# A two-layer decoder on one core: values of the first attention inside its heads, Toeplitz rows in the first stage, the convolution's operands and more of the early projection in the feed-forward

## What is computed

```python
# layer 0, attention (H = 16 heads of 16)
g = x @ Wg.T + bg
v = x @ Wv.T + bv
corr = dot(g, g) / (nrm_i * nrm_j + 1e-08)       # per head, masked to j <= i
corr = (corr + 1.0) / 2.0
denom = mean(corr, axis=3) + 0.5
gene_fitness = 1.0 / (denom * sum(1.0 / denom, axis=2))
attn = softmax(corr * gene_fitness[..., None] * m + (1.0 - m) * NEG)
out = (attn @ v) @ Wo.T + bo

# layer 1, moving average of the normalised input (p, a, q: 256 x 16)
p, a = sigmoid(ema_delta), sigmoid(ema_alpha)
q = 1.0 - p * a
kern = p * ema_beta * exp(t * log(q))
k_dl = einsum('dnl,dn->dl', kern, ema_gamma * sqrt(1 / 16))
conv = causal convolution of xn with k_dl over the 32 steps of t
mx = silu(conv + xn * ema_omega)

# layer 1, cross-attention: keys and values of the context
k = (K @ Wk.T + bk)          # 4096 x 1024
v = (V @ Wv.T + bv)          # 4096 x 1024
```

## Time and profile before

| what | us |
|---|---|
| median of three runs | 2650.11 (2647.54 to 2652.91) |
| the profiled execution | 2642.07, its span 2640.2 |
| projection | 0 to 80.4 |
| heads | 80.4 to 495.2 |
| cross-attention of layer 0 | 495.2 to 868.2 |
| feed-forward | 868.2 to 1000.1 |
| convolution | 1000.2 to 1212.8 |
| gated attention and all behind it | 1212.8 to 2640.2 |

### The profile page before, as it was taken

One profiled execution on the slowest core, in us unless ns is written; L12 is line 12 of the kernel. 1 busy time (PEld: TensorE's weight loads), 2 busy tenths in 40 slices (PEclk: granted clock), 3 DMA queues, 4 the chain that ended last, 5 costly groups with the idle time before them and its releaser, 6 DMA issues. The chain is left out here.

```text
span 2640.2 us, 44590 instructions
## 1 busy us (share of the span) xinstructions
PE 2322.6 (88%) x17186; PEld 1783.3 (68%) x17186; DVE 1347.6 (51%) x2515; ACT 1131.5 (43%) x1934; POOL 845.9 (32%) x881
## 2 busy tenths in 40 slices
PE   9688888699998778698989869999999699999994
...
GB/s 76 79 103 121 122 102 131 92 33 25 31 67 17 182 195 225 128 210 136 32 32 64 24 130 54 111 113 101 99 120 91 216 203 181 180 198 173 183 223 140
DMA packets 212481, 313.23 MB, mean 119 GB/s; under 512 B 63792, under 2 KB 194736, under 8 KB 198960
## 3 DMA queue, kind: packets, MB, share of 16 engines
...
## 5 line engine op out<-in xcount | busy, mean ns | idle before, releaser
L2653 ACT ACTIVATE me_h<-me_ps_h 128x512 f32<-128x512 f32 (+1 forms) x160 | 88.7, 554 | 423.8 <-PE me_ps_h L2631 423.8
L2694 DVE TENSOR_SCALAR me_yo<-me_ps_y,moe_xg 128x256 f32<-128x256 f32 x72 | 34.9, 484 | 422.8 <-PE me_ps_y L2641 369.1
L2567 POOL DMA_INDIRECT xo<-me_yo,me_row x72 | 112.7, 1565 | 410.2 <-DVE me_yo L2694 349.2
L2631 PE MATMUL me_ps_h<-me_xt,me_w 128*128 128x256 f32 (+1 forms) x1056 | 210.0, 357 | 0.0
L2641 PE MATMUL me_ps_y<-me_w,me_h 128*128 128x256 f32 x944 | 209.2, 379 | 0.7 <-DVE me_yo L2694 0.7
L2076 POOL TENSOR_TENSOR l1x_e<-l1x_e,l1x_ri 128x1024 f32<-128x1024 f32 x64 | 121.7, 1901 | 235.5 <-DVE l1x_ri L2360 235.5
L2641 PEld LDWEIGHTS me_ps_y<-me_w,me_h 128*128 128x128 f32 x944 | 179.0, 190 | 24.8 <-issue 1.1
L2631 PEld LDWEIGHTS me_ps_h<-me_xt,me_w 128*128 128x128 f32 x1056 | 182.0, 191 | 20.0
L664 POOL TENSOR_TENSOR l0x_e<-l0x_e,l0x_ri 128x1024 f32<-128x1024 f32 x64 | 120.0, 1896 | 202.7 <-DVE l0x_ri L893 202.7
L2195 PE MATMUL l1x_ps_p<-l1x_xct,l1x_w_q 128*128 128x256 f32 x512 | 122.3, 383 | 0.3 <-ACT l1x_xct L2281 0.3
L2233 PE MATMUL l1x_ps_o<-l1x_w_o,l1x_ot 128*128 128x256 f32 x512 | 118.8, 385 | 1.4 <-ACT l1x_ot L2306 1.4
(11 more groups left out here) (421 smaller groups left out, 5543.7 us busy)
## 6 DMA issues: line engine op xcount, KB each, us to landing
...
```

Of the source, the lines that this page charges most:

```text
L2567: pool.indirect_dma_start(token_rows, bass.IndirectOffsetOnAxis(row[:, j % 2, q:q + 1], 0), yo[:, j % 2, q, :], None, compute_op=ALU.add). ...
L2631: last = pe.matmul(ps_h[i % HB][:, f % 2, 0:P * size(j)], weights(j)[:, FFN * c + f * P:FFN * c + f * P + P], xt[:, j % 2, c, 0:P * size(j ...
L2653: act.activation(h[:, j % 2, 2 * i:2 * i + 2, 0:P * size(j)], ps_h[i % HB][:, :, 0:P * size(j)], ACT.Gelu).then_inc(gelued, 1)
```

## The change

Five things are changed together.

- `l0_attn_project` multiplies by the weights of g alone, 256 columns, with x in four slots. `va`, `w_v` and `b_v` move to `l0_attn_heads`, which transposes x itself (`transpose_x`), copies it on ScalarE (`copy_xv`), multiplies (`project_v`) and adds the bias on VectorE (`add_v`), into a ring of four tiles of v; x has a ring of five.
- The parameters of the moving average are loaded in the first stage, and the rows `kp` are worked out there, spread over tiles 12 to 22. SyncE stores them in the heads, one of 32 shifted stores in each step.
- The norms are inverted in four parts, three of them in the loop; the logarithm goes before the square root. Identity in bf16, mask, `lpad` and `rpad` are made in the first stage.
- In the heads the orders of GpSimd, VectorE, TensorE and ScalarE are written anew.
- A class `ConvolutionInput` holds blocks and input of the convolution from the feed-forward on. There GpSimd clears the blocks, and SyncE loads them and, group by group, the input. `FFN_STEP` is 7, so 78 pieces are left for the convolution stage: 6 ahead, one behind each of the 16 batches, 56 at the end. The gated attention's buffers `x`, `x2`, `ut`, `ub`, `xt` and `vb` are views of the two tiles.

```diff
@@ l0_attn_project
-        w = kit.sb("w", [P, 2, 2 * D])
-        x = kit.sb("x", [P, 2, D])
+        w = kit.sb("w", [P, 2, D])
+        x = kit.sb("x", [P, 4, D])
@@ scalar
+                def sigmoids():
+                    act.wait_ge(coef_loaded, 5 * 16)
+                    act.activation(pa[:, :, :, :], prm[:, 0:2, :, :], ACT.Sigmoid).then_inc(sig_done, 1)
+                def logarithms():
+                    act.wait_ge(q_done, 1)
+                    act.activation(q[:, 2, :, :], q[:, 1, :, :], ACT.Ln).then_inc(log_done, 1)
+                def exponentials():
+                    act.wait_ge(arg_done, 1)
+                    act.activation(ex[:, :, :, :], arg[:, :, :, :], ACT.Exp).then_inc(exp_done, 1)
+                unrolled(TILES, [(0, copy_xt), at_tile(12, sigmoids), at_tile(16, logarithms), at_tile(20, exponentials)])
                 act.wait_ge(clamped, 1)
+                act.activation(lg[:, :, :], n2[:, :, :], ACT.Ln).then_inc(logged, 1)
+                act.wait_ge(inverted, TILES // CHUNK)
                 act.activation(rn[:, :, :], inv[:, :, :], ACT.Sqrt).then_inc(rooted, 1)
-                act.wait_ge(clamped, 2)
-                act.activation(lo[:, :, :], n2[:, :, :], ACT.Ln).then_inc(logged, 1)
@@ vector
+                unrolled(TILES, [(0, add_bias), (1, sum_squares), (2, last_of_chunk), at_tile(14, decays), at_tile(18, powers), at_tile(22, kernel_rows)])
@@ l0_attn_heads, gpsimd
-                walk([(-2, pads), (1, lambda n: mask_e(n, 0)), (1, lambda n: mask_e(n, 1)), (2, last_of_group(roots)), (0, bias_x), (0, weigh_odd)])
+                walk([(2, bias_x), (3, last_of_group(roots)), (1, weigh_odd), (-2, pads), (1, lambda n: mask_e(n, 0)), (1, lambda n: mask_e(n, 1))])
@@ sync
-                unrolled(TILES, [(0, load), (1, clear), (8, store)])
+                def store_toeplitz(l):
+                    sp.dma_start(toep[l, :, :].rearrange("(h p) n -> p h n", p=P),
+                                 kp[:, :, L - 1 - l:2 * L - 1 - l]).then_inc(toep_stored, 16)
+                unrolled(TILES, [(0, load), (1, clear), (2, store_toeplitz), (8, store)])
@@ vector
-                walk([(1, weigh_even), (0, lambda n: correlate(n, 1)), (2, divide), (0, row_sums), (2, residual), (-1, lambda n: correlate(n, 0)), (0, fitness)])
+                walk([(1, weigh_even), (0, add_v), (0, lambda n: correlate(n, 1)), (2, divide), (0, row_sums), (2, residual), (-1, lambda n: correlate(n, 0)), (0, fitness)])
@@ tensor
+                def transpose_x(n):
+                    item_done(pe, x_loaded[n % XR], n // XR, 16)
+                    item_done(pe, ops_copied, n, 2)
+                    slot_free(pe, v_biased, n, 1)
+                    for k in range(2):
+                        last = pe.transpose(ps_a[1][:, k, :], x[:, n % XR, k * P:(k + 1) * P], ident[:, :])
+                    last.then_inc(xv_ready, 1)
+                def project_v(n):
+                    item_done(pe, xv_copied, n)
+                    for k in range(2):
+                        last = pe.matmul(ps_a[1][:, 2:4, :].rearrange("p a b -> p (a b)"), xvt[:, n % 2, k * P:(k + 1) * P], w_v[:, k, :],
+                                         start=k == 0, stop=k == 1)
+                    last.then_inc(v_ready, 1)
@@ scalar
-                walk([(0, copy_ops), (2, lambda n: exponentials(n, 1)), (0, lambda n: guard(n, 0)), (7, normalise), (2, copy_et), (0, lambda n: guard(n, 1)), (1, lambda n: exponentials(n, 0))])
+                walk([(8, normalise), (2, lambda n: exponentials(n, 1)), (0, lambda n: guard(n, 0)), (0, copy_xv), (2, copy_et), (0, lambda n: guard(n, 1)), (1, lambda n: exponentials(n, 0)), (-1, copy_ops)])
@@ l0_ffn
-FFN_FIRST, FFN_STEP = 10, 5
-CONV_AFTER = 40
+FFN_FIRST, FFN_STEP = 10, 7
+CONV_FIRST, CONV_PIECES = 6, 1
@@ sync
-                for s in range(1, NG + 3):
+                for s in range(1, NG + 4):
...
+                    if 0 <= s - 5 < cv.G:
+                        cv.load_blocks(sp, s - 5)
+                    if 0 <= s - 4 < NG:
+                        load_rows(s - 4)
@@ mega_conv, tensor
-                kv.make(pe, first, first + CONV_AFTER)
-                pe.wait_ge(x_loaded, 16 * G)
-                pe.wait_ge(t_loaded, 16 * G)
+                kv.make(pe, begin, among)
+                pe.wait_ge(cv.t_loaded, 16 * G)
+                pe.wait_ge(cv.x_loaded, 16 * G * TILES // 4)
...
-                    if i % 2:
-                        kv.make(pe, first + CONV_AFTER + i // 2, first + CONV_AFTER + i // 2 + 1)
+                    kv.make(pe, among + CONV_PIECES * i, among + CONV_PIECES * i + CONV_PIECES)
```

384 lines of the change are left out of this document (211 added, 173 removed).

## The result

The changed kernel takes 2707.33 us, median of four runs (2707.06 to 2708.98); the kernel before took 2651.51 beside it (2647.54 to 2654.84, four runs). The ratio is 1.0212, interval 1.0195 to 1.0230: slower by 56 us, where 45 us less was forecast. That it is slower is clear; whether by more than 2% the interval leaves open. The profiled execution of after took 2708.98 with a span of 2706.5, that of before 2642.07 with 2640.2.

The account below looks back on a forecast made before the run. It put the whole-program wait chain in the unchanged expert stage and read early stages by their busiest engine, mainly TensorE, with GpSimd holding the feed-forward. -28.2 + 9 + 22 - 48 = -45.2 gave 2605 us (2593 to 2616).

Parts of the forecast that it names:

- Projection, forecast -28.2: Stage one: halved product, Toeplitz rows added, shorter end and earlier clears sum to -28.2 us (-21 to -33).
- 3.9 + 2.4: End of stage one: chunked reciprocals and earlier logarithm save 3.9 us, clears and mask moved to the start save 2.4.
- Heads, forecast +9: Heads: value work moved there costs +6 us over 29 steady tiles and +3 at the start (0 to +20).
- The steady +0.2 a tile: Heads: TensorE's row grows 1.33 us, mostly absorbed by existing holes, leaving +0.2 us a tile (0 to +0.4).
- Feed-forward, forecast +22: Feed-forward: two more pieces a step cost +18 us and SyncE's loads at the end +4 (+10 to +32).
- its last term: Feed-forward's end: SyncE's eight remaining row loads, less about 1 us of GpSimd's lag, cost +4 us (+1 to +9).
- 98.6 + 2 forecast: Feed-forward: seven steps of 12.8 us plus five holes of 1.8 make 98.6, plus 2 for one clock fall.
- the five of 1.8: Feed-forward's five middle steps: TensorE waits 1.8 us in each for ScalarE before the third late piece.
- Rival C: Feed-forward: the clock oscillates, every hole followed by a fall, 13 us more, 2618 us; chance 0.10.
- Convolution, forecast -48: Convolution stage: 16 pieces fewer (26.2 us) and no Toeplitz block stall (21.8); -44 if ScalarE is late.
- Rival B: Feed-forward: transfers choke it, the last four steps each waiting 5 us more, 2625 us; chance 0.10.
- The rule weighed: Feed-forward: clock-gate rule that a loop waiting every round drops to 1.2 GHz; five holes would each cost 3 us.

Follow-up runs that it names:

- e1: Changed kernel with the convolution's input loaded by four loads of 32 time steps at the convolution stage's start, none in the feed-forward; 2599.46 us.
- e3: Changed kernel with its 32 row loads as 32 time steps by 16 batch rows, read from network input x without the store wait; 2582.36 us.
- e3c: Changed kernel with its loads of 4 time steps by 128 rows kept, but read from network input x without the store wait; 2711.55 us.
- b1: e1 with 20 pieces instead of 6 ahead of the convolution's first batch; 2584.97 us, ratio 0.9773 to the kernel before.
- e7: b1 with five pieces instead of seven in each feed-forward step; 2594.23 us.
- e4: Changed kernel with 16 row loads of 8 time steps instead of 32 of 4; 2632.88 us.
- e5: Two kernels: e3 with one of each four loads cut into 31 + 1 time steps, 2621.84 us, or into 30 + 2, 2580.73 us.
- b2: e1 with 32 loads of 32 time steps by 16 rows from xn and 16 pieces ahead; 2586.03 us, ratio 0.9759 to the kernel before.
- b3: e1 with 24 pieces instead of 6 ahead of the convolution's first batch; 2579.98 us, ratio 0.9749 to the kernel before.

## Why the prediction was wrong

- **Projection, forecast -28.2, measured -28.4: right, by its own terms.** The start gained 2.4 (1.5 forecast). 31 tiles of 1.08 would take 33.5 us and took 40.4, so the Toeplitz rows and reciprocals cost 6.9 (6). The end gained 6.4 (3.9 + 2.4). In seven of the twelve experiments this same code ends some 3 us later (the first fill at 57.6 to 59.1 instead of 55.2 to 55.8), so the exact hit is in part luck.
- **Heads, forecast +9, measured +0.9 with the cross-attention: the small number is luck.** The steady +0.2 a tile was right (0.18, 29 tiles, 5.2), and so, in this profile, was the start: from the first fill to the fifth 38.1 us instead of 34.5 (+3.5, +3 forecast), though the clock there was 0.57 and not the 0.50 of the earlier trace rows. The heads up to the cross-attention (495.20 before, 469.85 after) grew by 3.0 all the same, because the profile of before has two tiles of 17.4 and 14.7 us instead of 11.5. In each TensorE stands without anything that the profile shows it to wait for, and its clock is lower afterwards (0.52 in the window 342 to 349, 0.72 in 381 to 386); neither stands in the profile of after. Without these 9 us the heads would have cost some 12. The two rows of before:

```profile
342.47 0.48 PE L463 MATMUL l0ah_ps_a<-l0a_ident,l0ah_rpad 128*128 128x128 f32 x1 [2.95 <-issue]
...
381.10 0.33 PE L462 MATMUL l0ah_ps_a<-l0a_ident,l0ah_lpad 128*128 128x128 f32 x1 [2.37 <-issue]
```

From the first fill to the feed-forward the 13 profiles of the changed code take 780.0 to 788.5 us (after 785.4), so one profile can't tell +9 from 0 here. The cross-attention's -2.1 was not looked into.
- **Feed-forward, forecast +22, measured +143.4: wrong.** The step that failed is its last term, SyncE's loads at the end, "+4 (+1 to +9)". It priced only the last eight of 32 loads and put the other 24 at nothing, without a reason. Its two ends (0.71 and 12.1 us) are from the earlier trace rows, where a load has 32 time steps, so the loads of four steps were given the speed of another form. The last eight held SyncE 33.4 us, the other 24 held it 115.0, 4.8 us each in the median. They stood ahead of a load and of the stores for which ScalarE, VectorE and GpSimd wait (61 us), and they ran on when all engines had done (66 us). e1 takes them out (-129.8 in this stage), e3 changes their form and source (-126.8), e3c puts the form back with the source kept (+125.3 in this stage).
- **The rest of the feed-forward's forecast was right.** In e3 and b1 the seven steps take 98.5 us, 98.6 + 2 forecast, and e7 shows that two pieces a step less bring 81.8. The holes were smaller than the five of 1.8 (0.84 to 1.31), but one of 2.12 was followed by a piece of 3.52 us instead of 1.9, half clock. Where that fall stays away (e4, both e5, b2) the steps take 96.8. Rival C, a fall behind every hole, did not come. With the loads' end at +0.7 instead of +4, e3's stage is +16.6.
- **Convolution, forecast -48, measured -48.3: right**, without a wait, and with the store 66.3 us in (67).
- **Rival B had the place, not the size.** "The transfers choke the feed-forward" took the queue's 12 us and four steps of 5, 20 us at a chance of 0.10. It named no waiting instruction and no transfers behind the last work. Worked out, its link was on hand: the stores of `xn` are behind the loads on SyncE, and GpSimd has two slots.
- **The rule weighed** was the clock's, and it bore on 2 us. The case of the Trainium skill, "TensorE: Matmul & The Clock Gate", section "HAM oscillation — how this bites in real kernels", is a loop that waits longer in each round than it works. The steps here work 12.8 us and wait 1 to 2, so the prediction carried the rule too far. The 15 us of rival B came from the table in the Trainium skill, "DMA: Bandwidth & Descriptors", section "Bandwidth", and that table is for loads into 128 partitions. The rule on the outermost dimension, quoted under e5, stands on the same page and was not asked: 4 here, 32 in the form that was taken as the price. What bore on 140 us is this and the few partitions.
- Without the miss (e3, span 2580.3) the change would have been 59.9 under before, 14.7 more than the forecast's 45.2: 8 from the heads (the two stalls of before are 9), 5.4 from the feed-forward, 1.2 from the rest. e3 computes other numbers; b3, which computes the right ones, has a span of 2579.5.
